# Tile 7's quantised product directly behind tile 6's, and norm 3's first six transposes in one row

## The reference

```
x = x + attention(layernorm(x))                       # one head of 256, Wqkv, Wo
x = x + fake_quant(layernorm(x)) @ fake_quant(ctx)    # ctx (2, 1024, 1024), 8-bit grid, here on an exact bf16 grid
xf = layernorm(x)
inter = xf @ c1.T @ c2.T                              # rank 16, then 3584 columns, blocks of 64
idx = argmax within each block of 64                  # 56 chosen rows of w1 and w2t per token
x = x + sum_k relu(w1[idx_k] . xf) * w2t[idx_k]
```

## Time and profile before

| | us |
|---|---|
| median of 3 runs (lowest, highest) | 771.0 (770.23, 771.32) |
| the profiled execution, its own time | 770.48 |
| its span, first to last instruction | 768.6 |
| TensorE matmul busy in the span | 762.0 (99%) |
| VectorE / GpSimd / ScalarE busy | 613.8 / 468.8 / 247.3 |

### The profile page before, as it was taken

The page is one execution under the profiler, slowest core; times in us unless marked ns, Lnnn a source line. Parts: engine busy times, 40 slices in busy tenths (PEclk is TensorE's granted clock), DMA queues, the critical chain, the costliest instruction groups (busy, mean ns, idle before and its releaser), DMA issues.

```text
span 768.6 us, 11457 instructions
## 1 busy us (share of the span) xinstructions
PE 762.0 (99%) x3586; PEld 625.1 (81%) x3586; DVE 613.8 (80%) x974; ACT 247.3 (32%) x378; POOL 468.8 (61%) x306
## 2 busy tenths in 40 slices
PE   8999999999999999999999999999999999999998
PEld 8888887478888888888888888888888888888887
DVE  5888769998887878888878788787888787778864
ACT  6347668884132120303121221203031212222120
POOL 4878898779997264646547363636464563737260
PEclk9999999999999999999999999999999999999999
DMA  9536405300222221222222222212122222222114
GB/s 319 209 109 217 171 6 156 60 15 1 69 68 71 67 70 22 68 73 68 75 68 68 75 68 68 68 53 60 44 68 75 68 75 68 68 68 68 61 38 194
DMA packets 59636, 64.19 MB, mean 84 GB/s; under 512 B 41312, under 2 KB 43616, under 8 KB 59360
## 3 DMA queue, kind: packets, MB, share of 16 engines
q1 hardware_dynamic: 59328, 62.75, 26.0%
q10 hardware_dynamic: 288, 1.18, 0.4%
HBM read 50.79 MB, written 4.19 MB: 72 GB/s over the span
## 4 chain that ended last, share of the span: by engine, by line
PE 92%; DVE 4%; ACT 2%; DMA 1%; issue 1%; SPq 0%; DVEq 0%; ACTq 0%
PE bank L1911 13%; PE bank L1912 13%; PE bank L1913 13%; PE bank L1811 12%; PE bank L1812 12%; PE bank L1813 12%; PE bank L1618 4%; PE bank L1620 4%; PE bank L1619 4%; PE bank L1802 2%; DMA x<-x_in 1%; DVE x L1302 1%; PE bank L1781 1%; DVE xn L1289 1%; ACT spread L775 1%
## 5 line engine op out<-in xcount | busy, mean ns | idle before, releaser
L1911 PE MATMUL bank<-w_hi,h_hi 128*128 128x512 f32 (+1 forms) x450 | 175.5, 390 | 0.0
L1912 PE MATMUL bank<-w_lo,h_hi 128*128 128x512 f32 (+1 forms) x450 | 175.3, 390 | 0.0
L1913 PE MATMUL bank<-w_hi,h_lo 128*128 128x512 f32 (+1 forms) x450 | 174.7, 388 | 0.0
L1415 DVE TENSOR_TENSOR x<-bank,x 128x512 f32<-128x512 f32 x207 | 132.7, 683 | 48.2 <-PE bank L1913 48.2
L638 POOL TENSOR_TENSOR lo_r<-r,slot 128x512 fp32r<-128x512 f32 x54 | 70.9, 1314 | 158.0 <-ACT slot L882 158.0
L1913 PEld LDWEIGHTS bank<-w_hi,h_lo 128*128 128x128 f32 x450 | 84.5, 188 | 18.0
L1911 PEld LDWEIGHTS bank<-w_hi,h_hi 128*128 128x128 f32 x450 | 84.5, 188 | 17.3 <-POOL w_lo L643 0.3
L1912 PEld LDWEIGHTS bank<-w_lo,h_hi 128*128 128x128 f32 x450 | 84.7, 188 | 15.0
L1811 PE MATMUL bank<-xT_hi,slot 128*128 128x512 f32 x232 | 90.5, 390 | 0.0
L1812 PE MATMUL bank<-xT_lo,slot 128*128 128x512 f32 x232 | 90.3, 389 | 0.0
L946 ACT ACTIVATE h_hi<-bank 128x512 fp32r<-128x512 f32 x56 | 33.4, 600 | 118.9 <-DVE bank L1356 81.4
(11 more groups left out here) (212 smaller groups left out, 1595.0 us busy)
## 6 DMA issues: line engine op xcount, KB each, us to landing
r<-w SPq DMA_DIRECT2D x56, 256.0 KB, 3.4
w_raw<-w SPq DMA_DIRECT2D x28, 512.0 KB, 4.0
x<-x_in SPq DMA_DIRECT2D x8, 512.0 KB, 10.7
ctx_raw<-ctx_in SPq DMA_DIRECT2D x8, 512.0 KB, 3.5
xn<-ctx_in SPq DMA_DIRECT2D x8, 512.0 KB, 4.5
out<-x SPq DMA_DIRECT2D x7, 512.0 KB, 2.6
W_raw<-wqkv SPq DMA_DIRECT2D x6, 512.0 KB, 10.9
xT_raw<-xT_in SPq DMA_DIRECT2D x1, 2048.0 KB, 19.7
```

The source lines that it names most:

```text
L1415: nc.vector.tensor_tensor(x[:, t, c], bank[unit_banks(g)[p]][:, :], x[:, t, c], ALU.add).then_inc(unit_added, 1)
L1911: nc.tensor.matmul(dst, h_hi[:, j, m], w2_hi[:, j, c], start=j == 0, stop=False)
L1912: nc.tensor.matmul(dst, h_hi[:, j, m], w2_lo[:, j, c], start=False, stop=False)
L1913: last = nc.tensor.matmul(dst, h_lo[:, j, m], w2_hi[:, j, c], start=False, stop=j == GJ - 1)
```

## The change

TensorE makes tile 7's product directly behind tile 6's, and then the transposes of tiles 0 to 5 in one row. The job list follows: the product of tile 7 takes the banks 4 and 5, the transposes of tile 0 the banks 0 and 1, those of tile 1 the banks 2 and 3; all later jobs keep their numbers and banks. VectorE adds tile 7's product before the remainders of tiles 0 and 1 rather than behind them. ScalarE makes tile 6's variance before the evictions of tiles 0 and 1 rather than behind them.

```diff
@@ job_order
     jobs += both("CB", 0) + both("WO", 6) + both("XA", 0) + both("CB", 1) + both("WO", 7) + both("XA", 1)
-    for t in range(2, 7):
+    for t in range(2, 8):
         jobs += both("XA", t)
-    jobs += both("T3", 0) + both("T3", 1) + both("XA", 7)
-    for t in range(2, 6):
+    for t in range(6):
         jobs += both("T3", t)
     jobs += [("U", 0)] + both("T3", 6) + both("T3", 7)
@@ ScalarE's program
             variance(2, 5)
             roots(2, 4)
+            variance(2, 6)
             hi_first(0)
             hi_first(1)
-            variance(2, 6)
             plain_hi(0, 1)
             plain_hi(0, 2)
             hi_first(2)
@@ VectorE's program
             add_XA(6)
             norm_scale(2, 4)
+            add_XA(7)
             lo_T(2, 0)
             lo_T(2, 1)
-            add_XA(7)
             lo_T(2, 2)
@@ TensorE's program
-            for t in range(2, 7):
+            for t in range(2, 8):
                 quantised_product(t)
-            transpose_norm(2, 0)
-            transpose_norm(2, 1)
-            quantised_product(7)
-            for t in range(2, 6):
+            for t in range(6):
                 transpose_norm(2, t)
             rank_projection(0)
```

## The result

The changed kernel takes 772.85 us in the median of 8 runs (771.96 to 774.23), the kernel before, run beside it, 770.58 (8 runs, 770.10 to 771.32): a ratio of 1.003, 95% interval 1.002 to 1.0039. The whole interval lies above 1, so the kernel is slower, by 0.3%. The profiled execution took 772.31 us, with a span of 770.4 against 768.6, at a mean granted clock of 1.000.

What follows compares the result with a forecast made beforehand. ScalarE's row of evictions was taken to bound the projection: first eviction 2.89 us later, less 1.13 for the variance, gives +1.76, so 771.0 + 1.76 = 772.8 us. Range 771.9 to 773.7, or 771.0 to 774.2 with rivals 2 and 4.

Steps and rivals of the forecast that it cites:

- What bounds the kernel: Before the rank projection: ScalarE's row of evictions, not busy-reading TensorE, sets the projection's start, 165.81 in the kernel before.
- Tile 7's product: On TensorE behind tile 6's product: starts at 156.14 with no wait, so tile 0's transposes start at 159.60.
- The start of the row: ScalarE's first eviction: 0.64 us behind tile 0's first transpose, at 160.24, 2.89 us later than before.
- The variance hidden: Tile 6's variance on ScalarE before the first eviction: cost 0, gain 1.13 us, with 0.7 us of cover.
- The row's length: ScalarE from first eviction to end of tile 3's copy: 7.62 us less 1.13 leaves 6.49, ending at 166.73.
- Tile 5's transposes: On TensorE ahead of the projection: nearest rival bound, ending near 167.0, 0.5 us before the projection's turn, hidden.
- GpSimd's normalisations of tiles 4 and 5: Tile 4's waits for tile 0's transposes at about 160.6; they end at 161.9 and 163.1, before TensorE wants them.
- The sum: Projection at 167.57 against 165.81, +1.76 us (2.89 - 1.13), with nothing behind it giving the delay back.
- The clock: In TensorE's row of 48 transposes: expected to stay up, as the opening's transposes suggested; a fall kept as a rival.
- Rival 3: TensorE's clock falls in the row of transposes or its waits: 2.9 us lost, sum +4.7, some 775.7; chance 4%.
- The median: Whole kernel: 771.0, the median of the runs shown, + 1.76 = 772.8 us.

Runs made afterwards that it cites:

- run 2: Changed kernel with tile 6's variance put back on ScalarE between the evictions of tiles 1 and 2: 775.25 us, ratio 1.006.
- run 3: Changed kernel with ScalarE's two roundings of w1 moved from between tiles 1 and 2 to between tiles 2 and 3: 773.55 us.
- run 4: Changed kernel with the two roundings of w1 moved ahead of the first eviction, into ScalarE's idle gap: 771.66 us, ratio 1.001.
- run 5: Kernel before with only tile 6's variance moved ahead of the first eviction on ScalarE: 771.07 us, ratio 1.0009.
- run 6: Kernel before with tile 6's variance moved behind tile 5's evictions and both roundings of w1 behind tile 3's: 771.49 us.
- run 7: Kernel before with one rounding of w1 moved from ahead of tile 2's evictions to behind tile 3's: 770.31 us, ratio 0.9999.
- run 8: Run 2's kernel with 20 more identity transposes into an unused bank ahead of tile 5's transposes: 773.15 us.
- run 10: Changed kernel unaltered, measured beside run 9 on the same chip: 773.32 us.
- run 9: Changed kernel with ten more identity transposes ahead of tile 5's transposes: 772.24 us, ratio 1.0019.

## Why the prediction was right, and where not

- **What bounds the kernel: right.** Runs 2, 3 and 4 moved the end of tile 3's copy by +1.11, 0.00 and -0.82, and the distance by +1.11, 0.00 and -0.83, with TensorE's order untouched. In every one of the twelve traces the projection starts 0.84 or 0.85 us behind the end of that copy, whatever was moved. In us from the start of tile 6's product:

  | kernel | first eviction | end of tile 3's copy | projection |
  |---|---|---|---|
  | before | 4.67 | 12.29 | 13.13 |
  | changed | 7.56 | 14.07 | 14.92 |
  | run 2 | 7.55 | 15.18 | 16.03 |
  | run 3 | 7.56 | 14.07 | 14.92 |
  | run 4 | 7.79 | 13.25 | 14.09 |
  | run 5 | 6.75 | 13.23 | 14.08 |
  | run 6 | 4.68 | 12.16 | 13.01 |
  | run 7 | 4.69 | 12.18 | 13.02 |

- **Tile 7's product: right.** It runs on behind tile 6's with no wait; transposes start 159.70 - 152.78 = 6.92 us behind tile 6's start, as 2 x 3.46 said.
- **The start of the row: right.** Transpose to first eviction 160.34 - 159.70 = 0.64, the value taken from tile 6's evictions. The first eviction came 2.99 us later, 2.89 with the 0.10 taken off.
- **The variance hidden: right**, with 0.70 us of cover as forecast; and its worth there is 1.11 (run 2).
- **The row's length: right.** 6.49 forecast, 166.85 - 160.34 = 6.51 measured (the chain's later starts included). Tile 5's transposes were the nearest other bound, and stayed hidden, by less than forecast: they end at 166.33 + 1.16 = 167.49, 0.21 us ahead of the projection and not 0.5.
- **GpSimd's normalisations of tiles 4 and 5**: from 160.91 for 2.38 us, forecast 160.6 to 163.1. Hidden.
- **The sum: +1.76 forecast, +1.79 in the trace**, and kept to the end of the span.
- **The clock: the chance was mis-sized.** Rival 3 was held to be a case of 4% that either comes or doesn't, worth 2.9 us. It comes in half of the executions and is worth 1.5 to 1.6. The argument against it was that transposes count for the clock. Run 8 bears that out. Its ground in the opening is weaker than it was put: the granted clock reads 1.00 in both stretches there, and only the durations speak for a rise. And it answered the wrong question: the harm is not in the 48 transposes, but in the waits between them, which the prediction had counted (2.7 us, of which the trace shows 0.31 + 1.33 + 0.21 = 1.85 as waits) and priced at nothing but delay. The projection itself then pays. The price of 2.9 us, taken from the opening, was too high as well: the low level lasts some 3 us here and costs half of that.
- **The median: 772.8 forecast, 772.85 measured, and partly by luck.** From the 770.58 of the runs beside it, +1.79 makes 772.37, which is where the executions at full clock are (median 772.22). The other 0.5 us is there because every second execution has the drop. The 0.4 us by which the three runs shown at first (771.0) lay above the eight (770.58) filled its place.

## What to carry to other kernels

An engine that reads 99% busy can still be released by another one at every step of a stretch: follow the chain of waits through the stretch, and move work only after asking which engine's row will start later for it. A wait in the busiest engine's list is not a cost by itself; a step that shifts it to the next wait shows that (run 3). And a side operation in a critical row may be filling a gap: the same move of 1.13 us lost 0.95 in one order and gained 1.11 in the other.

Keep the pieces of standing still between bursts of TensorE short, or fill them. Look at the mean clock of every execution and not only at the profiled one; two groups of times whose medians lie 1.5 us apart, the upper one at a clock of 0.997 or 0.998, were such a drop here.

## What the runs showed of the hardware that I had not expected

TensorE's clock fell to its lower level (granted 0.50) behind waits of 0.30, 1.33 and 0.21 us with short transposes between them in the trace of run 10, and behind 0.31, 2.45 and 0.21 us in that of run 2. By the mean clock such a drop came in 11 of 22 executions of the changed kernel and in 5 of 5 of run 2. It also came in 3 of 5 of run 3, whose trace (of an execution without a drop) has waits of 0.30, 0.31 and 1.23, and in none of 11 of run 4, with 0.30, 0.30 and 0.21. Why the same kernel has it in one execution and not in the next stays open. The full level was granted again while TensorE worked without a pause, from 171 us on in the last trace. Transposes of the identity into an unused bank, put where TensorE waited, kept the mean clock at 0.999 or more in 16 of 16 executions (runs 8 and 9), without lengthening the distance. The page "TensorE: Matmul & The Clock Gate" of the Trainium skill, section "Part 4: PE-mode transpose", says that transposes don't count as busy for the clock; runs 8 and 9, with f32 transposes, differ from it.
